# Frame merging and input projection in one block: the projection's first chunks and taps stand between the last frame steps, and its loops are written out

## What is computed

```python
h = _L0_tok_ref(x, Wq, bq, Wkv, bkv)                   # frame merging
u = _layernorm(_layernorm(h), ln_w, ln_b)
zxbcdt = u @ W_in                                      # projection, 192 -> 1030
z, xBC, dt = zxbcdt[..., :384], zxbcdt[..., 384:1024], zxbcdt[..., -6:]
xBC = silu(causal_dw_conv(xBC, conv_w, conv_b))        # 4 taps
dt = softplus(dt + dt_bias); A = -exp(A_log)
...                                                    # state space, y * silu(z), W_out
```

## Time and profile before

| | |
|---|---|
| median of 3 runs | 592.81 us (591.47 to 593.81) |
| the profiled execution's own time | 597.21 us |
| its span, first to last instruction | 595.1 us |
| busy share of the span | PE 89%, PEld 79%, DVE 50%, ACT 42%, POOL 37% |
| mean granted TensorE clock | 0.929 of 2.4 GHz |

### The profile page before, as it was taken

The page is one execution under the profiler, slowest core; times in us unless marked ns, Lnnn a source line. Parts: engine busy times, 40 slices in busy tenths (PEclk is TensorE's granted clock), DMA queues, the critical chain, the costliest instruction groups (busy, mean ns, idle before and its releaser), DMA issues. The chain is left out here.

```text
span 595.1 us, 12563 instructions
## 1 busy us (share of the span) xinstructions
PE 531.8 (89%) x4135; PEld 472.0 (79%) x4135; DVE 295.7 (50%) x932; ACT 249.0 (42%) x678; POOL 222.8 (37%) x332
## 2 busy tenths in 40 slices
PE   8999799988999729999999999997977737999995
PEld 7677678876887628999999999995977736999975
DVE  2666458777999883233223322322456544333330
ACT  2677656664554232222322232222345541545422
POOL 1244400004997503222112211203877215566731
PEclk9999669998999859999999999997799976999989
DMA  9990000009742101131311311111344321222210
GB/s 259 251 187 4 1 1 1 0 12 287 237 130 77 42 2 48 41 81 50 85 41 42 90 45 42 41 34 47 107 120 147 88 73 47 61 61 61 67 43 24
DMA packets 42701, 45.74 MB, mean 77 GB/s; under 512 B 7665, under 2 KB 37058, under 8 KB 42642
## 3 DMA queue, kind: packets, MB, share of 16 engines
q1 hardware_dynamic: 35682, 31.30, 19.2%
q0 software_dynamic: 6000, 12.30, 7.7%
q10 hardware_dynamic: 960, 1.38, 0.8%
HBM read 29.39 MB, written 10.32 MB: 67 GB/s over the span
## 5 line engine op out<-in xcount | busy, mean ns | idle before, releaser
L1374 POOL DMA_INDIRECT rows_in<-x,token x57 | 57.1, 1002 | 151.6 <-PE psum L1399 126.9
L1420 PE MATMUL psum<-rows_turned,expert_weights 128*128 128x128 f32 x684 | 86.9, 277 | 1.1 <-issue 0.6
L1438 PE MATMUL psum<-w_proj,hidden_room 128*128 x468 | 86.2, 334 | 0.0
L1420 PEld LDWEIGHTS psum<-rows_turned,expert_weights 128*128 128x128 f32 x684 | 81.7, 193 | 2.1 <-issue 1.4
L1438 PEld LDWEIGHTS psum<-w_proj,hidden_room 128*128 128x128 f32 x468 | 75.0, 190 | 4.6
L1461 ACT ACTIVATE hidden_room<-psum 128x384 f32<-128x384 f32 x78 | 34.0, 488 | 76.6 <-PE psum L1424 76.6
L1495 DVE COPY rows_out<-psum 128x192 f32<-128x192 f32 x39 | 13.9, 358 | 104.0 <-PE psum L1438 104.0
L1424 PE MATMUL psum<-rows_turned,expert_weights 64*128 64x128 f32 x684 | 54.9, 292 | 0.0
L1450 ACT ACTIVATE rows_turned<-psum 128x256 f32<-128x256 f32 x57 | 22.1, 388 | 76.0 <-PE psum L1399 70.2
L1424 PEld LDWEIGHTS psum<-rows_turned,expert_weights 64*128 64x128 f32 x684 | 43.8, 189 | 7.1 <-issue 0.2
L714 PE MATMUL psum<-arena 97*128 (+3 forms) x192 | 48.1, 415 | 0.6 <-PEq L403 0.6
(11 more groups left out here) (269 smaller groups left out, 988.0 us busy)
## 6 DMA issues: line engine op xcount, KB each, us to landing
xbc_tile<-xbc SPq DMA_DIRECT2D x16, 320.0 KB, 3.2
w_proj<-in_w_proj SPq DMA_DIRECT2D x8, 576.0 KB, 5.5
y<-rows_out SPq DMA_DIRECT2D x39, 96.0 KB, 1.6
sz<-in_x SPq DMA_DIRECT2D x16, 192.0 KB, 8.1
w_fc<-in_w_fc SPq DMA_DIRECT2D x1, 2304.0 KB, 19.9
w_fc<-in_w_fc SPq DMA_DIRECT2D x3, 768.0 KB, 25.4
w<-in_w SPq DMA_DIRECT2D x3, 576.0 KB
x<-xf_tile SPq DMA_DIRECT2D x16, 96.0 KB, 1.6
```

Source lines behind the costliest of these rows:

```text
L1374: nc.gpsimd.indirect_dma_start(out=x[:, t.odd, 0:D], out_offset=None, in_=src, in_offset=bass.IndirectOffsetOnAxis(ap=tile_token[:, t.i:t. ...
L1420: nc.tensor.matmul(ps_h[t.odd][ch // HALF][:, ch % HALF, :], w_now[:, t.odd, ch * P:(ch + 1) * P], xt[:, t.odd, 0, :], start=ch % HALF == ...
L1438: last = nc.tensor.matmul(ps_y[t.odd], hid[:, t.odd, ch, :], w_down[:, bass.ds((e * HC + ch) * D, D)], start=ch == 0, stop=ch == HC - 1)
```

## The change

The two blocks become one. `project_in` no longer opens a block; it returns functions that `merge_frames` calls in its engines' streams.

- TensorE: chunk n of stretch 0 is issued at the end of step 17 + n, for n = 0 to 5; chunks 6 and 7 after the last step, then stretches 1 to 3, written out. Each chunk waits for the last user of its bank: chunk 0 for `qk_ev` 15, chunk 2 (gate 0, bank 5) for `h_out` 16, chunks 3 to 5 for `s_min`, `pt_ev`, `c_ev` and `b_done`, chunk 6 for `ut_kept` and `ut_low` 16, chunk 7 for `dt_out` 16.
- The order of chunks changes from c0 c1 g0 c2 c3 g1 c4 g2 to c0 c1 g0 c2 c3 c4 g1 g2.
- ScalarE: `exp_A` goes to the start of the kernel; the first taps 0, 1, 2, 3 of stretch 0 go to the ends of steps 18, 19, 21, 22. After the steps come exp of dt, first tap 4, ln of dt, a one-column silu that loads the silu table, and `gate(0, 0)`. Then ScalarE runs a rotated order, in which `first_tap(j, c)` stands just behind `silu(j-1, c)`, so that `silu(j-1, 4)` no longer stands before `first_tap(j, 0)`.
- VectorE: taps 0, 1, 2 of stretch 0 go to the ends of steps 19, 20, 22; the softplus operations stand between taps 3 and taps 4; stretches 1 to 3 are written out.
- The second silu of `exp_A` with its wait for dt_A is gone, and so is one end of a block.

```diff
-            merge_frames(nc, dram, m, s, banks)
-            project_in(nc, dram, m, s, banks)
+            with ExitStack() as both:
+                merge_frames(nc, dram, m, s, banks, project_in(nc, m, s, banks, both))
...
+                def project_in(t):
+                    n = t.i - 9
+                    if n == 0:
+                        pe.wait_ge(ones_set, 1)
+                        pe.wait_ge(w_low, 4)
+                        pe.wait_ge(row_low, 2)
+                        pe.wait_ge(ut_low, 4)
+                        pe.wait_ge(qk_ev, TILES - 1)
+                    elif n == 1:
+                        pe.wait_ge(qk_ev, TILES)
+                    elif n == 2:
+                        pe.wait_ge(h_out, TILES)
...
+                    if 0 <= n < 6:
+                        projection.chunk(pe, 0, n)
...
+                ... (4, bias_row), (8, project_in)], 8, straight=True)
+                pe.wait_ge(ut_kept, TILES)
+                pe.wait_ge(ut_low, TILES)
+                projection.chunk(pe, 0, 6)
+                pe.wait_ge(dt_out, TILES)
+                projection.chunk(pe, 0, 7)
+                projection.tensor(pe)
...
+                def first_taps(t):
+                    c = {10: 0, 11: 1, 13: 2, 14: 3}.get(t.i)
+                    if c is not None:
+                        projection.first_tap(act, 0, c)
...
+                act.wait_ge(o_mm, TILES)
+                projection.scalar(act)
...
+                def other_taps(t):
+                    c = {11: 0, 12: 1, 14: 2}.get(t.i)
+                    if c is not None:
+                        projection.taps(dve, 0, c)
...
+                dve.wait_ge(m.loaded, 16)
+                dve.wait_ge(dt_out, TILES)
+                projection.vector(dve)
...
+    chunks = [("conv", 0, 3), ("conv", 1, 4), ("gate", 0, 0), ("conv", 2, 5), ("conv", 3, 6), ("conv", 4, 7), ("gate", 1, 1), ("gate", 2, 2)]
+    def tensor(pe):
+        for j in range(1, STRETCHES):
+            for n in range(len(chunks)):
+                chunk(pe, j, n)
+        pe.wait_ge(taps_done, 3 * (5 * (STRETCHES - 1) + 1))
+        stay_busy(nc, banks[0][:, 0:P], m.c["ident"], 28)
+    def scalar(act):
...
+        act.wait_ge(mag_done, 1)
+        act.activation(ex[:, :], mag[:, :], ACT.Exp, scale=-1.0).then_inc(exp_done, 1)
+        first_tap(act, 0, 4)
+        act.wait_ge(one_done, 1)
+        act.activation(ln1[:, :], one_ex[:, :], ACT.Ln).then_inc(log_done, 1)
+        act.activation(warm[:, :], p["A_log"][:, 0:1], ACT.Silu)
+        gate(0, 0)
+        for j in range(1, STRETCHES):
+            silu(j - 1, 0)
+            first_tap(act, j, 0)
+            gate(j - 1, 1)
+            silu(j - 1, 1)
+            first_tap(act, j, 1)
+            gate(j - 1, 2)
+            silu(j - 1, 2)
+            first_tap(act, j, 2)
+            silu(j - 1, 3)
+            first_tap(act, j, 3)
+            gate(j, 0)
+            silu(j - 1, 4)
+            first_tap(act, j, 4)
...
+    def vector(dve):
+        nc.vector.scalar_tensor_tensor(mag[:, :], m.dt[:, :], -1.0, m.dt[:, :], ALU.mult, ALU.max).then_inc(mag_done, 1)
+        taps(dve, 0, 3)
+        dve.wait_ge(exp_done, 1)
...
+        taps(dve, 0, 4)
+        dve.wait_ge(back2, 1)
+        dve.wait_ge(log_done, 1)
...
+        for j in range(1, STRETCHES):
+            for c in range(5):
+                taps(dve, j, c)
```

More of the change, by code:

```diff
@@ L333, in semaphore, with merge_frames @@
         return self.semaphores[-1]
-def merge_frames(nc, dram, m, s, banks):
+def merge_frames(nc, dram, m, s, banks, projection):
     with ExitStack() as ctx:
@@ L396, in merge_frames @@
             "qk_out", "least_score_ready", "exp_ready", "sum_inverted", "probs_ready", "h_bias_ready", "probs_t_out", "frame_mix_out"))
-        h_out, st1, mv1, ve1, roots_done, shift_set, u_out, ha = (sem(n) for n in (
-            "h_ready", "sums1", "mean_var1", "var_eps1", "roots_ready", "shift_ready", "u_ready", "h_plus_a"))
+        w_low, h_out, st1, mv1, ve1, roots_done, shift_set, u_out, ha = (sem(n) for n in (
+            "w_in_low_ready", "h_ready", "sums1", "mean_var1", "var_eps1", "roots_ready", "shift_ready", "u_ready", "h_plus_a"))
         ut_ev, ut_kept, ut_low, dt_out, w_high = (sem(n) for n in ("ut_out", "ut_high_ready", "ut_low_ready", "dt_out", "w_in_high_ready"))
@@ L501, in steps @@
                     last.then_inc(dt_mm, 1)
-                pipelined(pe, TILES, [(3, mix_frames), (6, turn_u), (7, steps), (1, score), (0, project), (2, turn_probs), (3, attend), (4, bias_row)], 8, straight=True)
+                def project_in(t):
[10 more added lines that the diff above has]
+                        pe.wait_ge(h_out, TILES)
+                    elif n == 3:
+                        pe.wait_ge(s_min, TILES)
+                    elif n == 4:
+                        pe.wait_ge(pt_ev, TILES)
+                    elif n == 5:
+                        pe.wait_ge(c_ev, TILES)
+                        pe.wait_ge(b_done, TILES)
+                    if 0 <= n < 6:
+                        projection.chunk(pe, 0, n)
+                pipelined(pe, TILES, [(3, mix_frames), (6, turn_u), (7, steps), (1, score), (0, project), (2, turn_probs), (3, attend), (4, bias_row), (8, project_in)], 8, straight=True)
+                pe.wait_ge(ut_kept, TILES)
[4 more added lines that the diff above has]
+                projection.tensor(pe)
             @block.scalar
@@ L513, in _ @@
                 act.wait_ge(params, 16)
+                projection.exp_a(act)
                 act.wait_ge(wv_mm, 1)
@@ L558, in row_high_part @@
                         act.activation(s.w_parts[HD:HD + 1, 0, 0, t.i * 512:(t.i + 1) * 512], ps_row[HD:HD + 1, :], ACT.Identity).then_inc(row_high, 1)
-                pipelined(act, TILES, [(5, norm), (5, add_normed), (6, take_u), (1, exponent), (2, take_probs), (3, take_h), (2, w_in_high), (4, row_high_part)], 8, straight=True)
+                def first_taps(t):
+                    c = {10: 0, 11: 1, 13: 2, 14: 3}.get(t.i)
+                    if c is not None:
+                        projection.first_tap(act, 0, c)
+                pipelined(act, TILES, [(5, norm), (5, add_normed), (6, take_u), (1, exponent), (2, take_probs), (3, take_h), (2, w_in_high), (4, row_high_part), (8, first_taps)], 8, straight=True)
+                act.wait_ge(o_mm, TILES)
+                projection.scalar(act)
             @block.vector
@@ L634, in w_in_low @@
                         dve.wait_ge(w_high, t.i + 1)
-                        nc.vector.scalar_tensor_tensor(s.w_parts[0:HD, 1, ch, at], w_in[:, ch, at], p["ln_w"][0:HD, ch:ch + 1], s.w_parts[0:HD, 0, ch, at], ALU.mult, ALU.subtract)
+                        nc.vector.scalar_tensor_tensor(s.w_parts[0:HD, 1, ch, at], w_in[:, ch, at], p["ln_w"][0:HD, ch:ch + 1], s.w_parts[0:HD, 0, ch, at], ALU.mult, ALU.subtract).then_inc(w_low, 1)
                 def row_low_part(t):
@@ L673, in _ @@
                 pipelined(pool, TILES, [(4, roots)], 8, straight=True)
[L676 to L778, removed]
-                dve.wait_ge(log_done, 1)
-                nc.vector.tensor_tensor(one_ex[:, :], ln1[:, :], mag[:, :], ALU.add).then_inc(back3, 1)
-                dve.wait_ge(back3, 1)
-                nc.vector.scalar_tensor_tensor(m.dt[:, :], m.dt[:, :], 0.0, one_ex[:, :], ALU.max, ALU.add).then_inc(sp_done, 1)
-                dve.wait_ge(sp_done, 1)
-                dve.wait_ge(ea_done, 1)
-                nc.vector.scalar_tensor_tensor(m.dt_a[:, :].rearrange("p (i h) -> p i h", h=NH), m.dt[:, :].rearrange("p (i h) -> p i h", h=NH), -1.0,
-                                               e_a[:, :].unsqueeze(1).to_broadcast([P, TILES, NH]), ALU.mult, ALU.mult).then_inc(a_done, 1)
-                def superblock(j):
-                    for c in range(5):
-                        full = pre[:, c, :].rearrange("p (b t) -> p b t", t=BLK)
-                        src = banks[c][:, :].rearrange("p (b t) -> p b t", t=BLK)
[L794 to L798, removed]
-                            nc.vector.scalar_tensor_tensor(full[:, :, back_by:], src[:, :, :BLK - back_by], p["conv_w"][:, 4 * c + 3 - back_by:4 * c + 4 - back_by],
-                                                           full[:, :, back_by:], ALU.mult, ALU.add).then_inc(taps, 1)
-                superblock(0)
-                with dve.Fori(1, N_TOK // SB) as j:
-                    superblock(j)
```

87 lines of the change are left out of this document (85 added, 2 removed).

## The result

The changed kernel took 589.75 us (median of 4 runs, 584.30 to 598.06), the kernel before 593.31 (591.47 to 595.36). The ratio is 0.9847, with a 95% interval from 0.9805 to 0.9889: 9 us faster. Eighteen executions of the changed kernel were timed in three batches. Against the median of the kernel before in the same batch (593.3, 593.1, 598.2) they lie at

The account below looks back on a forecast made before the run. TensorE was taken to bound the kernel, with idle time and half clock in the drain. Filling the drain was to end the block at 126.0 instead of 131.67, 5.6 us earlier: 592.81 - 5.6 = 587.2 us, range 583.5 to 591.5.

Parts of the forecast that it names:

- The main case: Seam between frame steps and projection: clock back at 75.4, TensorE's end 126.0 against 131.67, 5.6 us earlier; chance 0.42.
- TensorE ends the block: End of the projection: TensorE's unread transposes end at 131.67, 0.9 us after the other engines, and set the block's end.
- The prices: Drain steps and projection: a six-matmul chunk costs 1.39 us at full clock, 2.56 at half; late-case steps 19 to 21 take 3.85 each.
- The early case: Drain: clock back at 66.9 or never fallen, VectorE's queue the chain, end at 123.2, 8.5 us earlier; chance 0.28.
- the small wait of `steps` for dt: Last drained steps: `steps` 15 on TensorE waits for dt 14, starting at 80.85 in the main case.
- the wait for gate 0: Stretch 1's gate chunk: TensorE idles until ScalarE's gate(0, 0) frees its bank, 88.3 to 89.05, 0.7 to 1.5 us.
- The bound of the clock's return: Drain: after falling at 63.47, TensorE's clock returns between 66.9 and 83.95; the middle, 75.4, was taken.
- Its other premise: Drain: the clock fell at 63.47, before the first inserted chunk could start (64.8), so the change does not prevent the fall.
- The late case: Drain: clock back at 83.95 as before, gate at 92.4, end at 129.4, 2.3 us earlier, 590.5; chance 0.21.
- The slower rival: Mid-projection: the gate 0 wait sets off a second low stretch of 20.5 us, net 3.7 us slower, 596.5; chance 0.07.
- VectorE's waits: Projection loop turns: 1.46 us each, costing nothing before; without the rotation three would bring VectorE to 127.8, the bound.
- Past the seam, everything should only be shifted: Third block onward: profile expected unchanged except for starting earlier, its first instruction near 126.3.

Follow-up runs that it names:

- after_filled: Changed kernel plus unread 128-column matmuls: 4 at the end of step 16, 2 or 3 before each of chunks 0 to 5; 591.29 us, ratio 0.9883.
- filled_first_only: Changed kernel plus 4 unread matmuls at the end of step 16 alone, none before the chunks; 589.75 us, ratio 0.9877.
- again_2: The changed kernel timed a third time, no edit; 600.88 us against 598.16 for the kernel before, ratio 0.9843.
- before_dense: Kernel before plus six unread 512-column matmuls, like a conv chunk's, at the ends of steps 17 to 22; 611.38 us, ratio 1.0100.
- again: The changed kernel timed a second time, no edit; 596.76 us against 593.10 for the kernel before, no ratio given.
- before_filled: Kernel before plus 4 or 5 unread 128-column matmuls at the ends of steps 16 to 22; 592.49 us, ratio 1.0003.
- before_filled_rotated: Kernel before with those unread matmuls, ScalarE's rotated order, new chunk order and written-out loops, still two blocks; 593.79 us, ratio 0.9938.
- short_transposes: Changed kernel with 10 instead of 28 unread transposes at the end of the projection; 582.59 us, ratio 0.9796.

## Why the prediction came out as it did

The median of 589.75 lies in the range, but that is luck. The batch split three to three, the median is the middle between 584.65 and 594.85, and no execution came near it; the same kernel gave 596.76 and 600.88 in its other two batches. The ratio shows 9 us where 5.6 were forecast, and of eighteen executions none lies within 3 us of the forecast gain. The main case, a clock back at 75.4, was seen in no profile.

**TensorE ends the block: right.** 18 transposes fewer took 3.85 us off. **The prices: right.** A step with chunk was 3.85 us in the sum and is 3.84 in the profile.

**The early case: right in size, and nearly in mechanism.** Its sum has gate 0 at 86.15 and TensorE's end at 123.2. With the clock held high the gate ended at 85.86 and TensorE at 123.4 (after_filled), or at 85.48 and 122.9 (filled_first_only, which also shows the small wait of `steps` for dt, 0.40 us). Only the wait for gate 0 that the sum counts is hardly there: none in the first, under 0.1 us in the second. The six good executions lie 8.7 to 10.1 us under the kernel before, where 8.5 was written.

**The bound of the clock's return: wrong, and this is the step that failed.** The text says "the return is bounded by 66.9 and 83.95" and takes the middle. The three profiles of the changed kernel have it back at 89.2, 91.9 and 96.1 (the last with a drain that began late). I took the longest low stretch of the trace (20.5 us) as the end of the scale, but it is not a property of the stretch: in the kernel before, the clock rose 6.7 us after the projection's unbroken matmuls began (77.28 to 83.95). In seven other profiles it rose between 3.8 and 6.5 us after they began (85.47 to 89.24; 86.02 to 91.94; 90.95 to 96.12; 80.58 to 87.09; 84.99 to 89.64; 89.08 to 94.39; 77.19 to 81.85), and never among the drained steps. Putting a chunk into each step of the drain lengthens the drain at half clock from 77 to 85 us, and with it the wait for the rise. The change feeds the stretch that it was meant to fill. Its other premise, that the change does not prevent the fall, was no safer: in the changed kernel's profile the clock fell at 65.35, with the first chunk (64.96) already running, and whether it fell in the six good executions no profile shows.

What makes the clock rise stays open. Unbroken 512-column matmuls are not needed everywhere: in again_2 it rose at 48.34 after 13.66 us among the full frame steps, and in the changed kernel's profile at 195.06 after 6.83 us in the third block. TensorE was busy all through both, with matmuls of at most 192 columns.

"TensorE: Matmul & The Clock Gate", Part 1, of the Trainium skill says that activity releases the throttle. As a simple rule these profiles don't bear it out: the throttle was released after those 13.66 and 6.83 busy microseconds, but 30.42 busy microseconds of 30.72 went by at the low level in before_dense, where full chunks and small steps took turns.

**The late case: right rule, too short.** It gives TensorE's end at 129.4 for a return at 83.95, and each microsecond later costs 1 - 0.2315 / 0.427 = 0.46. For 89.24 that makes 131.8, measured 131.6 (125.15 + 6.41). For 91.94 it makes 133.1, as measured in again. For the 96.12 of again_2 it makes 135.0, where the third block began at 137.94; its whole drain ran late, which the rule doesn't hold.

**The slower rival** (a second low stretch in the projection, set off by the wait for gate 0) never appeared. TensorE didn't wait for gate 0 at all in the profile of the changed kernel. What keeps the gain from showing at the seam is the first stretch grown longer. That some of the twelve are slower than the kernel before is only in part its doing: the seam is at 131.83, 133.34 and 137.94 against 131.94, the last one late for the low stretch at 34.68 as well, and in the first the time is lost past the seam.

**VectorE's waits: right.** They cost nothing before and would have been the bound with a high clock: before_filled shows the one, before_filled_rotated the other.

**"Past the seam, everything should only be shifted": not quite.** The routing at the end of the third block (VectorE's last index lookup) ended 81.8 us after the block's start, against 75.3 before; the profile has an extra low stretch there, at 188.23. Three other kernels have one between 172.9 and 185.2 (short_transposes, filled_first_only, before_dense), and the same part of them lasts 80.8 to 82.8 us; the others have none and 75.8 to 78.8 us. before_dense doesn't have the change, so whether the change makes such a stretch more frequent stays open, and so does why after_filled still has three executions near the kernel before.

## What to carry to other kernels

Work put into a slack place is worth its full length only if the clock is up there; price it at both levels, and don't take the length of one low stretch as the time of the next return. If dense work is mixed into a chain of small steps at half clock, the chain gets longer and here the rise came later. Look at the spread of executions, too: two groups with a gap can be two courses of the clock, and one profile shows one of them. A few cheap matmuls ahead of the slack place (4 here, some 1.1 us) kept the clock up in every profile that had them. They are no cure: all six executions of filled_first_only were under the median of the kernel before, but of after_filled, with the same four and more, three of six were close to it.

## What the runs showed of the hardware

TensorE's granted clock stayed at 1.2 GHz for 24 to 31 us while the engine was busy in nearly all of them, with chunks of six 512-column matmuls between steps of 6 and 128 columns. It rose 3.8 to 6.7 us into the unbroken 512-column matmuls behind the steps. Elsewhere it rose without any: after 13.66 us of small matmuls in again_2, and after 6.83 us in the changed kernel's third block. Unread matmuls of 128 columns in the slack places, up to 1.4 us at a time, went with a clock of 2.4 GHz through the drain in all six filled profiles. A wait of 0.64 us near 33 us was followed by a fall in again_2 and by none in again and after_filled.
